# Graph attention with residual and layer norm: order of the setup in groups 0 and 1, width of the squares, place of a small product

## The reference

```python
in_fts = context @ W_common.T
left   = in_fts @ w_left  + b_left            # 8192
right  = in_fts @ w_right + b_right           # 8192
logits = left[:, None] + right[None, :]
logits = where(logits >= 0, logits, 0.2 * logits)
logits = where(adj <= 0, -inf, logits)
coefs  = softmax(logits, axis=-1)             # 8192 x 8192
y      = x + relu(coefs @ x)
out    = (y - mean(y)) / sqrt(var(y) + 1e-5)  # per row of 256
```

## Time and profile before

| | |
|---|---|
| runs | median 1493.46 us (1492.1 to 1494.03, three runs) |
| profiled execution | 1492.71 us, of which its span 1490.9 us and 1.8 us around it |
| busy share of the span | TensorE 92%, VectorE 88%, ScalarE 43%, GpSimd 6% |
| granted TensorE clock | 0.961 as a mean over the execution |
| HBM traffic | 329.59 MB by DMA, 221 GB/s |

### The profile page before, as it was taken

The page is one execution under the profiler, slowest core; times in us unless marked ns, Lnnn a source line. Parts: engine busy times, 40 slices in busy tenths (PEclk is TensorE's granted clock), DMA queues, the critical chain, the costliest instruction groups (busy, mean ns, idle before and its releaser), DMA issues.

```text
span 1490.9 us, 28348 instructions
## 1 busy us (share of the span) xinstructions
PE 1376.7 (92%) x12334; PEld 1209.7 (81%) x12334; DVE 1306.3 (88%) x1156; ACT 646.4 (43%) x691; POOL 82.1 (6%) x225
## 2 busy tenths in 40 slices
PE   1017999999999999999999999999999999999998
PEld 0014888888888888888888888888888888888887
DVE  6949999998989989998998989898998989899981
ACT  0267444444444344443444444444444444444441
POOL 0203000000000000000000000000000000000000
PEclk7558999999999999999999999999999999999999
DMA  9993998989898898989989898989988898988860
GB/s 380 304 250 99 237 233 215 236 213 236 221 230 227 214 235 213 231 221 232 230 221 226 207 245 206 234 219 238 225 212 235 207 229 220 238 219 221 207 171 9
DMA packets 81423, 329.59 MB, mean 221 GB/s; under 512 B 19728, under 2 KB 36112, under 8 KB 47504
## 3 DMA queue, kind: packets, MB, share of 16 engines
q1 hardware_dynamic: 79728, 321.47, 84.3%
q0 software_dynamic: 1568, 6.29, 1.5%
HBM read 319.29 MB, written 8.39 MB: 220 GB/s over the span
## 4 chain that ended last, share of the span: by engine, by line
PE 88%; SPq 4%; DVE 3%; DMA 3%; ACT 1%; issue 0%; POOL 0%; POOLq 0%; ACTq 0%; DVEq 0%
PE ps L362 29%; PE ps L365 29%; PE ps L363 29%; SPq L214 2%; DMA T<-in_x_dram 2%; DVE strip L672 1%; SPq L209 1%; DVE X L621 1%; SPq L237 1%; DMA strip<-in_adj_dram 1%; DVE T L718 1%; ACT ps L396 1%; ACT X L401 0%; ACT strip L432 0%; PE pt L336 0%
## 5 line engine op out<-in xcount | busy, mean ns | idle before, releaser
L362 PE MATMUL ps<-X,T 128*128 128x257 f16 x4096 | 1125.6, 275 | 7.5 <-ACT X L401 7.4
L363 PE MATMUL ps<-X,T 128*128 128x257 f16 x4096 | 1125.3, 275 | 0.0
L365 PE MATMUL ps<-X,T 128*128 128x257 f16 x4032 | 1101.6, 273 | 0.0
L432 ACT ACTIVATE strip<-strip 128x2048 f32<-128x2048 f32 x256 | 489.4, 1912 | 497.9 <-DMA strip<-in_adj_dram 497.5
L718 DVE STREAM_TRANSPOSE T<-strip 128x2048 f32<-128x2048 f32 x256 | 590.9, 2310 | 63.0 <-PE ps L365 63.0
L672 DVE SCALAR_TENSOR_TENSOR strip<-tab,arow,strip 128x2048 f32<-128x2048 f32 x256 | 598.6, 2339 | 52.5 <-ACT strip L432 51.0
L362 PEld LDWEIGHTS ps<-X,T 128*128 128x128 f16 x4096 | 403.2, 98 | 69.2 <-ACT X L401 16.2
L363 PEld LDWEIGHTS ps<-X,T 128*128 128x128 f16 x4096 | 403.3, 98 | 50.3
L365 PEld LDWEIGHTS ps<-X,T 128*128 128x128 f16 x4032 | 394.8, 98 | 49.2
L411 ACT ACTIVATE xs<-ps,small 128x256 f32<-128x256 f32 x64 | 30.3, 473 | 142.9 <-DVE small L723 142.7
L317 POOL TENSOR_SCALAR small<-small 128x1 f32<-128x1 f32 x64 | 12.2, 190 | 1270.8 <-ACT xs L419 1270.8
(11 more groups left out here) (93 smaller groups left out, 222.4 us busy)
## 6 DMA issues: line engine op xcount, KB each, us to landing
strip<-in_adj_dram SPq DMA_DIRECT2D x1016, 256.0 KB, 4.7
xs<-in_L_gnn_context_dram SPq DMA_DIRECT2D x14, 1024.0 KB, 9.7
T<-in_L_gnn_context_dram SPq DMA_DIRECT2D x4, 2048.0 KB, 17.3
X<-in_L_gnn_context_dram SPq DMA_DIRECT2D x4, 2048.0 KB, 33.7
xs<-in_x_dram SPq DMA_DIRECT2D x64, 128.0 KB, 5.2
out_dram<-xs SPq DMA_DIRECT2D x64, 128.0 KB, 5.1
gw<-in_L_gnn_context_dram SPq DMA_DIRECT2D x2, 1024.0 KB, 19.7
xs<-in_x_dram SPq DMA_DIRECT2D x4, 512.0 KB, 45.0
```

Of the source, the lines that this page charges most:

```text
L362: nc.tensor.matmul(ps[o][:, 0:D + 1], hi, X16[:, jb, 0:D + 1], start=(i == 0), stop=False)
L363: nc.tensor.matmul(ps[o][:, 0:D + 1], lo, X16[:, jb, 0:D + 1], start=False, stop=False)
L365: m = nc.tensor.matmul(ps[o][:, 0:D + 1], hi, X16[:, jb, XL:XL + D + 1], start=False, stop=(i == JB - 1))
L432: nc.scalar.activation(s, s, ACT.Relu, scale=KEEP).then_inc(s_m, 1)
```

## The change

- `SW = 8`: squares are summed over 8 rows at a time (8 instead of 16 instructions), and their unused output goes to the place of X instead of PSUM; the wait of each for the one before is gone. Since that output covers the ones columns, these are written later, between the steps of `x_factors`.
- ScalarE makes 44 high parts, `keep(4)`, 8 high parts, `keep(5)`, 12 high parts, `keep(6)`, `keep(7)`.
- VectorE makes 44 low parts, `masked(4)`, 8 low parts, `transposed(4)`, and then `masked` and `transposed` of strips 5, 6 and 7 in turn, and `masked(8)`.
- TensorE takes the three products of a block in the order `hi`·high, `hi`·low, `lo`·high.
- `spread_left(b)` moves from behind group 4b - 3 into group 4b - 2, behind block 16 of its 64.

The branch for general inputs follows along (it does not run here). No queue takes other DMAs or takes them in another order.

```diff
-    SW = 4
+    SW = 8
+        cut = [0, 44, JB - NPL, JB]
-        square_junk = psum2[:, :, :].rearrange("p b k -> p (b k)")
 ...
                     nc.tensor.matmul(ps[o][:, 0:D + 1], hi, X16[:, jb, 0:D + 1], start=(i == 0), stop=False)
-                    nc.tensor.matmul(ps[o][:, 0:D + 1], lo, X16[:, jb, 0:D + 1], start=False, stop=False)
                     if g > 0:
-                        m = nc.tensor.matmul(ps[o][:, 0:D + 1], hi, X16[:, jb, XL:XL + D + 1], start=False,
-                                             stop=(i == JB - 1))
+                        nc.tensor.matmul(ps[o][:, 0:D + 1], hi, X16[:, jb, XL:XL + D + 1], start=False, stop=False)
+                    m = nc.tensor.matmul(ps[o][:, 0:D + 1], lo, X16[:, jb, 0:D + 1], start=False,
+                                         stop=(g > 0 and i == JB - 1))
+                    if i == JB // 4 and g % LB == 2 and g // LB + 1 < NLB:
+                        spread_left(g // LB + 1)
 ...
                 m.then_inc(s_mm, 1)
-                if g % LB == 1 and g // LB + 1 < NLB:
-                    spread_left(g // LB + 1)
 ...
                 for j in range(XCH[c][0], XCH[c][1], SW):
-                    if j >= SW:
-                        act.wait_ge(s_ss, j // SW)
-                    nc.scalar.activation(square_junk, xrows(j, SW).rearrange("p j d -> p (j d)"), ACT.Square,
+                    nc.scalar.activation(Xflat[:, j * XW:j * XW + SW * D], xrows(j, SW).rearrange("p j d -> p (j d)"), ACT.Square,
                                          accum_out=SS[:, j // SW:j // SW + 1]).then_inc(s_ss, 1)
 ...
-                    if n < 2 * NB:
-                        for j in order[(n - NB) * 13:(n - NB + 1) * 13]:
+                    if n < NB + 3:
+                        for j in order[cut[n - NB]:cut[n - NB + 1]]:
                             high_part(j)
                     keep(n)
-                    if n == 2 * NB - 1:
-                        for j in order[NB * 13:JB]:
-                            high_part(j)
 ...
             def x_factors():
                 dve.wait_ge(s_ss, JB // SW)
                 nc.vector.tensor_reduce(ssx, SS[:, :], AX.X, ALU.max).then_inc(s_sc, 1)
+                nc.vector.tensor_scalar(X16[:, :, D], F[:, :], FSCALE, None, ALU.mult).then_inc(s_one_col, 1)
                 dve.wait_ge(s_bc, 2)
                 nc.vector.tensor_reduce(mxc[0:1, :], pt[0:1, P:2 * P], AX.X, ALU.max).then_inc(s_dg, 1)
+                dve.wait_ge(s_one_col, 1)
+                nc.vector.scalar_tensor_tensor(out=X16[:, :, XL + D], in0=F[:, :], scalar=FSCALE, in1=X16[:, :, D],
+                                               op0=ALU.mult, op1=ALU.subtract).then_inc(s_one_col, 1)
                 dve.wait_ge(s_all, 2)
 ...
-                    if n + 1 < NS and not SG - 1 <= n < 2 * SG:
+                    if n + 1 < NS and n >= 2 * SG:
+                        masked(n + 1)
+                    if n < SG - 1:
                         masked(n + 1)
                     if n == SG:
-                        one_columns()
                         x_factors()
                         dve.wait_ge(s_Fx, 1)
-                        for i in range(SG):
-                            for j in order[i * 13:(i + 1) * 13]:
-                                low_part(j)
-                            masked(n + i)
+                        for j in order[cut[0]:cut[1]]:
+                            low_part(j)
+                        masked(n)
+                        for j in order[cut[1]:cut[2]]:
+                            low_part(j)
                         dve.wait_ge(s_xl, JB - NPL)
                     transposed(n, n % NB, g, g % 2, k)
-                    if n == 2 * SG - 1:
+                    if SG <= n < 2 * SG:
                         masked(n + 1)
```

More of the change, by code:

```diff
@@ L583, in _ @@
             general = dve.value_load(flag.bitcast(I32)[0:1, 0:1])
[L585 to L589, removed]
             def second_left_dots():
@@ L593, in second_left_dots @@
                 for q in range(LB):
-                    left_dot(1, q, lctx01, Xflat[:, q % 2 * CIN:(q % 2 + 1) * CIN])
+                    left_dot(1, q, lctx01, Thalf[0][:, q % 2 * CIN:(q % 2 + 1) * CIN])
                     if q < LB - 1:
```

## The result

The changed kernel takes 1487.9 us (median of 8) where the kernel before takes 1493.9 in the same runs; the ratio is 0.9966, with a 95% interval of 0.9955 to 0.9977, or 5.1 us less (3.4 to 6.7). The medians alone would give 6.0 us, but single executions of either kernel spread over 3 to 4 us; one execution of the kernel before, of 2504.4 us, is left out of the ratio. The forecast was 3.9 us, 1489.5 as a time, in a range of 1487.6 to 1492.4. The measured median lies 0.3 us inside that range, and outside the 1488.3 to 1490.5 that the forecast had as its own.

What follows compares the result with a forecast made beforehand. TensorE's own rate was taken to bound the kernel from 175 us on, with late VectorE delaying group 2 before that. Starting group 2 earlier gave 173.21 - 169.15 - 0.15 = 3.9 us, so 1489.5, range 1487.6 to 1492.4.

Steps and rivals of the forecast that it cites:

- Step 1: Squares of x, before the high parts: they end at 102.15, 0.5 us earlier, with bounds of 0.3 and 1.2.
- (C): Rival on the squares: they give 1.2 us as the last chunk lands early, time 1488.8; chance 0.07.
- Step 2: Setup of groups 0 and 1 on ScalarE and VectorE: three waits go, group 2's last transpose ends at 169.12.
- Step 3: TensorE up to group 2: group 1, partly at 1.2 GHz, ends at 168.6; VectorE's 169.12 comes last, group 2 starts 169.15.
- Rival (B): TensorE around groups 1 and 2: a second lower-clock stretch costs 1.7 us, gain 2.2 to 2.7, about 1491.0; chance 0.13.
- by that rule: Skill page's clock rule for TensorE: waits between bursts lower the clock each time, making a second lower-clock stretch likely.
- Step 4: Small product: 0.25 us on the path ahead of group 2, 0.15 in mid-group; only b = 1 changes.
- Step 5: Order of a block's three products: 0.110 us each whatever follows, nothing taken; 1 ns a triple would be 4.0 us.
- Rival (E): TensorE's products: hi loaded twice in a row hides worse, 2 ns a triple costs 8.1 us, 1497.6; chance 0.06.
- (A): Strip loads in the setup: transfers stay the bound, masked(11) starts 2.4 later, gain 1.5 us, 1492.0; chance 0.10.
- (D): Start of group 2: nothing moves, it starts at 173 for a reason no row shows, 1493.5; chance 0.04.
- The sum: Whole kernel: 173.21 - 169.15 - 0.15 = 3.9 us gained by starting group 2 earlier, nothing behind it changing.

Runs made afterwards that it cites:

- changed, again: The changed kernel unaltered, run once more in a later set beside other variants; 0.9969 of the kernel before, median 1488.7 us.
- old products: The changed kernel with the three products of a block back in the old order (hi high, lo high, hi low); 0.9962 of the kernel before, median 1486.9 us.
- old place of small product: The changed kernel with the small product back ahead of group 2 (and 6, 10, ...); 0.9957 of the kernel before, median 1487.0 us.
- old squares: The changed kernel with squares of 4 rows into PSUM, each waiting for the one before; 0.9976 of the kernel before, median 1490.1 us.
- narrow squares: The changed kernel with 4-row squares, still into X's place and without the wait; 0.9971 of the kernel before, median 1489.6 us.
- setup alone: The kernel before with only the new setup order in group 1, and ones columns later; 0.9986 of the kernel before, median 1489.9 us.
- dots, not filled: The changed kernel with two dot products moved into VectorE's wait for keep(4), TensorE's pauses left unfilled; 0.9964 of the kernel before, median 1489.3 us.
- old setup: The changed kernel with the old order of high parts, low parts, masks and transposes in group 1; 0.9989 of the kernel before, median 1492.1 us.
- squares alone: The kernel before with only the 8-row squares into X's place and later ones columns; 0.9991 of the kernel before, median 1492.9 us.
- filled: The changed kernel with 17 and 15 useless products in TensorE's two pauses before group 1; 0.9963 of the kernel before, median 1489.8 us.
- filled, dots (two): The changed kernel with TensorE's pauses filled and two dot products in VectorE's wait for keep(4), run twice; 0.9961 and 0.9963, medians 1487.8 and 1487.9 us.

## Why the prediction was right, and where its sizes were off

The distances of all profiles, in us ("at half clock" counts products of group 1, to within one or two):

| kernel | third chunk used | squares | setup | at half clock | rest |
|---|---|---|---|---|---|
| before | 93.04 | 12.12 | 68.05 | 16 | 1317.7 |
| changed | 92.56 | 10.27 | 65.1 | 27 | 1317.8 |
| changed, again | 93.18 | 11.89 | 64.2 | 15 | 1317.8 |
| old products | 91.39 | 10.21 | 64.5 | 21 | 1317.8 |
| old place of small product | 91.74 | 11.44 | 64.5 | 14 | 1317.7 |
| old squares | 92.60 | 12.10 | 64.2 | 16 | 1317.8 |
| narrow squares | 94.74 | 11.04 | 64.5 | 21 | 1317.8 |
| setup alone | 92.14 | 12.12 | 65.4 | 28 | 1317.7 |
| dots, not filled | 96.13 | 10.20 | 64.6 | 22 | 1317.8 |
| old setup | 94.17 | 10.72 | 67.3 | 0 | 1317.8 |
| squares alone | 93.43 | 10.74 | 68.0 | 15 | 1317.7 |
| filled | 97.31 | 10.21 | 64.2 | 0 | 1319.3 |
| filled, dots (two) | 92.42, 93.85 | 10.23, 10.69 | 62.9, 62.9 | 0, 0 | 1317.9, 1317.8 |

The rest falls into two: 1317.7 in the four kernels that have the small product of b = 1 ahead of group 2, and 1317.8 to 1317.9 in the nine profiles that have it within group 2, the filled kernel aside.

**Step 1, the squares: right in kind, the term mis-sized.** It says that "the end is 102.15, 0.5 earlier". Measured is 1.9 with the chunk there, and 1.45 as a mean over the ten profiles with eight-row squares (10.66 against 12.11). The main fault is that I took the landing of the last chunk, 100.0, from one execution as if it were fixed. There it came 7.0 behind the third, and for such an execution 0.5 is about right: the last eight-row square starts at the landing and takes 2.04 to VectorE's reduction (98.30 to 100.34 in the changed kernel), as priced, so that I estimate the first high part at 104.6. In twelve of the other thirteen profiles it came sooner, 5.0 to 6.9 us behind the third. ScalarE waited for it in five of the ten profiles with eight-row squares, for 0.37 to 1.50, and in five not at all. The second fault is the step of the squares ahead of the last. I priced it at 2.05, from the old step with its wait; without the wait the accumulator read lies under the next square, and the step is 1.89 to 1.94. I had (C), with 1.2, at a chance of 0.07; it is nearer to the mean than my term. The rule on PSUM and SBUF, that ScalarE writes the first faster (the Trainium skill, "ScalarE: Activation LUTs", "Step-by-step: what each stage is for"), is borne out by the trace with 0.01 to 0.03 us for 1024 elements, which decides nothing.

**Step 2, the walk of VectorE: right.** It says 145.82 for the last transpose of group 1 and 169.12 for that of group 2, 41.16 and 64.46 behind the first high part. Measured are 41.12 and 64.12. The three waits went, and the old setup brought them back. The term under it holds too: I took 6.6 from a transpose to the `keep` of the strip that takes its buffer, and in the changed kernel it is 6.4, 6.4 and 6.7 for strips 8, 9 and 10.

**Step 3, TensorE until group 2: the pattern right, its size variable.** It says "I take the same: end at 168.6, half a us ahead of VectorE". The half clock came, at the start of group 1 rather than within it, for 14 to 28 products instead of 18. VectorE ends 64.1 behind the high parts, from which group 2 could start at 64.2; TensorE starts group 1 at 41.17 behind them and needs 21.1 plus 0.105 for each product at half clock, so 62.27 + 0.105 n. The larger of the two gives 65.1 for 27, 64.5 for 21, 64.6 for 22 and 64.2 for 15, 16 and none: within 0.1 of the rows of the table that have the new setup (setup alone and the old place of the small product have 0.15 to 0.3 for that in front). With the dots moved VectorE ends at 62.9, and TensorE without half clock at 62.3. From about 19 products on TensorE ends last. Rival (B) was at work in part, at 0 to 1.0 us, where I had given it 1.7 or nothing, and "either way VectorE's 169.12 comes last" did not hold: TensorE came last in five of the eight profiles with the pauses. That its cause is the pauses is shown by the filled kernels, 0 products in three profiles. Which of the two pauses it takes was not tested, and a pause alone does not decide it: those of 2.07, 2.02 and 3.27 us ahead of group 2 (before, squares alone, old setup) were each followed by full clock, granted 1.00 from there to 180. The page "TensorE: Matmul & The Clock Gate" of the Trainium skill, section "HAM oscillation — how this bites in real kernels", has each wait between short bursts of products bring the next burst back to the lower level. The trace agrees for group 1 and not for group 2, and the waits that the page describes are longer than the two pauses here, so that the prediction's "by that rule" took it further than it goes. The price here was at most 1.0 us, since VectorE hid the rest.

**Step 4, the small product: right.** 0.29 us and a step of 0.15 at 173.52, nothing in the later groups; undone, it moved the time by nothing that can be measured.

**Step 5, the order of the products: right.** With the old order put back, the rest, 12,000 products long, moved by less than 0.1. Rival (E) is out.

**The rivals (A) and (D)** are out for this kernel: strips 8 to 12 arrived ahead of their masks in every profile with the new order. VectorE does wait for a late strip further on, at strip 17: 1.6 to 5.7 us in the profiles with the new setup, but also 2.4 to 3.3 in the three with the old one, so the change did not bring this wait about. It cost TensorE 1.5 us in the one execution with the longest wait, and nothing in the others. I did not test what delays strip 17.

**The sum** was 3.9 and came out at 5.1 (3.4 to 6.7), so the term that was mis-sized is that of the squares: 0.2 to 1.9, 1.45 as a mean, where I had 0.5. The setup gave 3.0 to 3.9 where I had 3.56; the 0.15 for the small product goes off both. That the median of 1487.9 still lies in the range, by 0.3 us, is in part luck: the median of the kernel before alone moved from 1492.7 to 1494.6 between sets of runs. The single executions of the kernel before lie between 1490.7 and 1498.6 in one job, and the landing of x's third chunk between 91.4 and 97.3 over all profiles; since the rest of the path hangs on it as a whole, I take it for the main cause of that spread, which is argued and not shown, as single timed executions have no profile.

## What to carry to other kernels

When a buffer is freed by an instruction that stands in a row with its like, look at where in the queue the first of them could stand: the same 52 low parts, 4 masks and 4 transposes in another order ended 0.6 us later (41.1 behind the first high part, 40.5 before), and yet took 3.5 to 3.9 us of waits out of the next group. Price an instruction whose successor waits for it apart from one whose successor does not; the difference here, 0.14 of 1.18, came to 1.1 us over eight squares, more than the 0.8 that the wider tile saved. And when the last two engines to arrive are half a us apart, state both: filling TensorE's pauses alone moved the start of group 2 by 0 to 0.9 us and VectorE's wait alone by nothing, while both together moved it by 1.2 to 2.2.

## What was not expected of the hardware

Pauses of 1.8 to 2.5 and 1.4 to 1.8 us on TensorE, with half a us of products between them, were followed by a start at half clock in each of eight profiles; where products of no use filled them, there was none in three profiles. A single pause is less sure: of 2.11 and 2.35 us ahead of the last four products of group 0 it was followed by 16 and 15 products at half clock, of 2.43 by none, and pauses of 1.7 to 3.3 us ahead of group 2 by none in four profiles. The landing of one and the same chain of transfers differed by 5.9 us (91.39 to 97.31) between executions, though no kernel issues these loads in another order. ScalarE's square of 1024 elements took 1.04 to 1.06 into SBUF and 1.03 into PSUM.
